# One block of channels in four takes its input product on VectorE instead of through TensorE

## What is computed

```python
dbc = u @ W_x
delta = softplus(dbc[..., :dtr] @ W_dt + b_dt)           # (b, l, 256)
Bm, Cm = dbc[..., dtr:dtr + n], dbc[..., dtr + n:]        # (b, l, 16) each
deltaA = exp(einsum('bld,dn->lbdn', delta, A))
deltaBu = einsum('bld,bln->lbdn', delta * u, Bm)
h[l] = deltaA[l] * h[l-1] + deltaBu[l]
y[l] = einsum('bdn,bn->bd', h[l], C[l])
```

## Time and profile before

| | |
|---|---|
| median of three runs | 519.88 us (516.26 to 520.61) |
| profiled execution, its own time | 519.67 us |
| span of the core in it | 517.9 us, granted TensorE clock 0.938 |
| busy: TensorE, ScalarE, VectorE, GpSimd | 426.4, 334.5, 299.1, 253.7 us |
| first scan starts, last scan ends | 62.9 us, 369.6 us |

### The profile page before, as it was taken

The page is one execution under the profiler, slowest core; times in us unless marked ns, Lnnn a source line. Parts: engine busy times, 40 slices in busy tenths (PEclk is TensorE's granted clock), DMA queues, the critical chain, the costliest instruction groups (busy, mean ns, idle before and its releaser), DMA issues.

```text
span 517.9 us, 6511 instructions
## 1 busy us (share of the span) xinstructions
PE 426.4 (82%) x2021; PEld 255.3 (49%) x2021; DVE 299.1 (58%) x600; ACT 334.5 (65%) x736; POOL 253.7 (49%) x230
## 2 busy tenths in 40 slices
PE   5988888878979869888958688877796888999992
PEld 3432443343445334544524454533384576887881
DVE  0301554558564549855655986789668257553365
ACT  4235689795769795577797386996186298543242
POOL 2001074469555659557667757695654144332012
PEclk9998999989999979899997697989998799999997
DMA  8001700104100102301000412662120000000003
GB/s 249 13 0 46 197 25 22 41 1 120 45 22 20 41 2 51 96 28 34 20 21 2 124 41 103 209 234 107 50 113 1 2 0 1 1 2 1 1 33 130
DMA packets 18710, 29.11 MB, mean 56 GB/s; under 512 B 2698, under 2 KB 10676, under 8 KB 18420
## 3 DMA queue, kind: packets, MB, share of 16 engines
q1 hardware_dynamic: 18676, 28.70, 17.8%
HBM read 22.27 MB, written 2.23 MB: 47 GB/s over the span
## 4 chain that ended last, share of the span: by engine, by line
PE 36%; ACT 15%; issue 9%; DVE 8%; POOL 7%; POOLq 0%; DVEq 0%; ACTq 0%
PE bank L522 6%; ACT loop_buf L1009 6%; PE bank L657 5%; POOL state L1545 4%; PE bank L538 4%; ACT front_a L1019 3%; PE bank L833 3%; DVE state L1171 3%; PE bank L809 3%; PE bank L603 2%; ACT state L1043 2%; ACT state L1044 1%; PE bank L841 1%; PE bank L800 1%; PE bank L612 1%
## 5 line engine op out<-in xcount | busy, mean ns | idle before, releaser
L1171 DVE TENSOR_TENSOR_SCAN state<-front_a,bank 128x512 f32<-128x512 f32 x128 | 151.2, 1209 | 102.2 <-PE bank L522 62.3
L522 PE MATMUL bank<-ident,loop_buf 128*128 128x128 f32 x512 | 90.9, 299 | 40.1 <-ACT loop_buf L1009 33.3
L522 PEld LDWEIGHTS bank<-ident,loop_buf 128*128 128x128 f32 x512 | 63.0, 149 | 109.5 <-issue 37.3
L1009 ACT ACTIVATE loop_buf<-copy,b_rows 128x256 f32<-128x256 f32 x252 | 105.3, 496 | 0.1
L1545 POOL TENSOR_TENSOR state<-state,c_own 128x1024 f32<-128x1024 f32 x32 | 75.2, 2359 | 50.3 <-DVE state L1171 50.3
L1545 POOL TENSOR_TENSOR state<-state,front_a 128x1024 f32<-128x1024 f32 x32 | 79.9, 2510 | 37.9 <-DVE state L1171 37.9
L1019 ACT ACTIVATE front_a<-loop_buf,a_neg 128x512 f32<-128x512 f32 x128 | 84.4, 712 | 10.9 <-DVE state L1171 9.9
L657 PE MATMUL bank<-state,fold 128*64 128x512 f32 x256 | 75.5, 671 | 10.2 <-POOL state L1545 6.1
L538 PE MATMUL bank<-front_c,conv_raw 128*128 128x512 f32 x128 | 60.4, 603 | 2.9 <-ACT front_b L884 1.2
L538 PEld LDWEIGHTS bank<-front_c,conv_raw 128*128 128x128 f32 x128 | 22.9, 195 | 23.7 <-issue 20.4
L1562 POOL TENSOR_TENSOR loop_buf<-state 128x256 f32<-128x256 f32 x24 | 17.8, 742 | 30.3 <-DVE state L1316 30.3
(11 more groups left out here) (197 smaller groups left out, 681.6 us busy)
## 6 DMA issues: line engine op xcount, KB each, us to landing
front_a<-c_stage SPq DMA_DIRECT2D x32, 128.0 KB, 2.9
c_own<-c_stage SPq DMA_DIRECT2D x32, 128.0 KB, 2.9
loop_buf<-front_b SPq DMA_DIRECT2D x32, 128.0 KB, 2.4
copy<-in_L_attn_x SPq DMA_DIRECT2D x4, 512.0 KB, 4.9
front_b<-in_L_ffn_wo SPq DMA_DIRECT2D x1, 2048.0 KB, 9.0
copy<-in_L_ffn_wq SPq DMA_DIRECT2D x1, 2048.0 KB, 9.6
out<-loop_buf SPq DMA_DIRECT2D x3, 512.0 KB, 2.9
conv_raw<-in_L_attn_conv_w SPq DMA_DIRECT2D x2, 512.0 KB, 3.7
```

The source lines that it names most:

```text
L522: return pe.transpose(dst, src, ident[:])
L1009: act.activation(zed[:, g % NZ, c, :, i, :], du_rows[b % 2][:, c, :].rearrange("p (k d) -> p k d", k=2 * KD), ACT.Copy, scale=b_rows[:, b ...
L1171: dve.tensor_tensor_scan(state[:, t % NH, j, :], decay[:, u % NDA, :], bank[BU_BANK[u % NBU]][:], 0.0, ALU.mult, ALU.add).then_inc(scanned, 1)
```

## The change

The fourth block of channels (k = 3, channels 192 to 255) no longer goes through Z and a bank:

- Z has three blocks: each Z activation has 192 elements instead of 256, and TensorE skips `turn_bu` for k = 3. Each of the three banks now belongs to one k, so that `turn_bu(u)` waits for `scan(u - 4)` instead of `scan(u - 3)`.
- VectorE makes the product itself (`make_bu`, L1213 of the new kernel): one 128x512 `tensor_tensor` of `b_wide` and `du_wide`, both in SBUF, in place, once a pair, after the first scan of the pair. The fourth scan reads both of its operands from SBUF.
- `b_wide` holds B broadcast over the partitions: two more transfers of 128 KB for each pair, behind the two for C (`widen_bc`). `du_wide` holds delta*u of the last 64 channels twice: two transfers for each batch (`widen_du`), behind the eight of `widen_delta`.
- To make room `duT` and `x_rows` have one copy instead of two, so that loading x for a batch waits for the transposes of the x before.

```diff
-        silu_r, uT, resT, du_rows, duT, x_rows = ([copies[i][1][j] for i in range(2)] for j in range(6))
+        silu_r, uT, resT, du_rows = ([copies[i][1][j] for i in range(2)] for j in range(4))
+        duT, x_rows = copies[0][1][4:]
...
+        b_wide = copies[1][0][:, 4 * KD * L:].rearrange("p (s l) -> p s l", s=NCW)
...
                 if b >= 1:
                     wait_filled(sp, ("xT1", b - 1))
...
+            def widen_du(b):
+
+                if b >= 2:
+                    sp.wait_ge(bu_made, NPAIR * (b - 1))
+                sp.wait_ge(du_ready, KD * (b + 1))
+                for i in range(2):
+                    sp.dma_start(du_wide[i * P // 2:(i + 1) * P // 2, b % 2, :],
+                                 duT[P // 2:, KD - 1, :]).then_inc(in_du[b % 2], 16)
...
+                if g >= NCW:
+                    sp.wait_ge(scanned, 4 * (g - NCW + 1))
+                for i in range(2):
+                    sp.dma_start(b_wide[i * P // 2:(i + 1) * P // 2, g % NCW, :],
+                                 bc_stage[b, 2 * m + i:2 * m + i + 1, :].partition_broadcast(P // 2)).then_inc(in_b[g % NCW], 16)
...
             def turn_bu(u):
                 g, k = u // 4, u % 4
-                if u >= NBU:
-                    pe.wait_ge(scanned, u - NBU + 1)
+                if k == KZ:
+                    return
+                if g >= 1:
+                    pe.wait_ge(scanned, u - 4 + 1)
...
+            def make_bu(g):
+
+                b = g // NPAIR
+                dve.wait_ge(in_b[g % NCW], 32 * (g // NCW + 1))
+                dve.wait_ge(in_du[b % 2], 32 * (b // 2 + 1))
+                dve.tensor_tensor(b_wide[:, g % NCW, :], b_wide[:, g % NCW, :], du_wide[:, b % 2, :], ALU.mult)\
+                   .then_inc(bu_made, 1)
...
             for t in range(B * NST):
                 scan(2 * t)
+                if t % 2 == 0:
+                    make_bu(t // 2)
                 scan(2 * t + 1)
```

80 lines of the change are left out of this document (50 added, 30 removed).

## The result

| | before | after |
|---|---|---|
| median of four runs each, side by side | 518.14 us (516.26 to 520.61) | 532.50 us (527.46 to 537.47) |
| profiled execution, its own time | 519.67 us | 530.28 us |
| span, granted TensorE clock | 517.9 us, 0.938 | 528.5 us, 0.905 |
| up to the first scan; the loop; behind it | 62.9; 306.6; 148.4 us | 60.65; 318.8; 149.1 us |

The changed kernel is slower: ratio 1.0244, 95% interval 1.0184 to 1.0305 (that it is slower by more than 2% is not shown by this). Ratios here are taken over undisturbed executions only, so one can differ a little from the quotient of two medians. The profiled executions differ by 10.6 us: 2.3 less ahead of the loop, 12.2 more in it, 0.7 more behind it.

What follows compares the result with a forecast made beforehand. No engine was full in the loop: VectorE set ten dense pairs, while in the 22 others scans waited for TensorE and ScalarE. Sum: 519.7 + 2.2 + 16 + 0 - 11 = 526.9, so 527 us; range 510 to 545.

Steps and rivals of the forecast that it cites:

- An added wait for GpSimd: VectorE's product and SBUF scan in the loop wait for a running GpSimd operation; 31.5 us of waits in all.
- Rival (2): In the loop, a scan from SBUF doesn't wait for GpSimd, giving 519.5 us; chance 0.17.
- The product's waits: Behind each pair's first scan, the product waits for GpSimd: 8.4 us over 32 places, product mean 0.95 us.
- The ten dense pairs: Ten loop pairs with VectorE busy 76.2 of 79.5 us; product and waits add 16 us there, between 11.2 and 27.4.
- the end read at the places: Low end for the ten pairs VectorE fills: 14.5 us of product and waits less 3.3 idle, 11.2 us.
- The 22 other pairs: Remaining loop pairs, with 97.7 us of VectorE idle time against 39 us of new work: 0 us added.
- The far end of 13: A third of the 39 us in the 22 pairs is passed on if later scans hold up other engines: 13 us.
- SyncE, 2.2: Ahead of the loop, B's transfers stand before those that widen delta, making the first scan 2.2 us later.
- Removed: Loop work taken from TensorE (22.7 us of transposes) and ScalarE (13.4 us of Z); 11 us gained, between 5 and 25.
- (1): VectorE's idle time in the loop swallows the new work, so the kernel gets faster, 510 us; chance 0.16.
- (3): VectorE and GpSimd become the bound in every loop pair, 7.75 us before front or tail work; 551 us, chance 0.15.
- (4): The product waits for its transfers at three batch starts, 3 us or so each; 536 us, chance 0.07.

Runs made afterwards that it cites:

- full_path: Changed kernel with nothing removed: Z has four blocks, all transposes are made, product and SBUF scan stay, B has two slots; ratio to before 1.0442.
- product_only: Same as `full_path`, but the fourth scan reads its bank again, so the product is made and not used; ratio to before 1.0133.
- after_again: The changed kernel itself, unaltered, timed once more beside `to_bank`; 535.48 us, ratio to before 1.0309.
- to_bank: Changed kernel with the product written into the PSUM bank the pair's first scan has just read, and the fourth scan reading it there; 520.37 us, ratio 0.9989.
- slot: Changed kernel with the last two scans of a pair exchanged, so the SBUF scan is third; ratio to before 1.0218.
- x_late: Kernel before, with only the load of x of batch 1 moved behind the router weights and the first transpose of x; 520.45 us.
- b_behind: Changed kernel with B's first transfers, for four pairs, issued behind those that widen delta; ratio to before 1.0226.
- to_bank_late: As `to_bank`, with the product one place later, directly behind the second scan; 519.83 us, ratio to before 1.0051.

## Why the prediction was right, and where its sum was not

The direction, the range and the mechanism were right: 527 forecast, 510 to 545, slower at 0.54; 530.28 in the profiled execution and 532.5 by the median. That the number came so near is in part luck. The loop was to grow by 16 + 0 - 11 = 5 us and grew by 12.2; the first scan was to come 2.2 us later and came 2.3 earlier, by a clock that was not forecast; behind the loop 0.7 came in. 7.2 - 4.5 + 0.7 is the 3.4 us between 526.9 and 530.3. By its steps:

**"An added wait for GpSimd"** is shown, and for the scan too. Forecast were means of 1.9 us for SBUF scans and 1.21 for the others, measured 1.925 and 1.209. `full_path` against `product_only` and `after_again` against `to_bank` put the scan's wait at 16 and 15 us, the largest single part of the change. Rival (2), that a scan from SBUF doesn't wait, is refuted. The rule weighed there, from "SBUF — State Buffer" of the Trainium skill, section "Who interferes with whom", holds here for a scan with 2.55 us beside a `weigh` of 2.36 and 1.20 without one. The runs add that of two instructions which one release sets free together VectorE's can come first, as at 132.33 in `slot`.

**The product's waits** were read as 8.4 us at fixed places and are 38.6 - 32 x 0.668 = 17.2. The scans' came out at 61.6 - 32 x 1.20 = 23.2 against 23.1. The places moved: in a stretched pair a `weigh` begins with each first scan, and the product finds half of it left, as in the pair at 137.80. The mean was to be 0.95 and is 1.21.

**The ten dense pairs, 16**: the term is for the added work alone, and so `full_path`, which removes nothing, measures it: 13.0 (6.0 for the product, 6.9 for the SBUF scan). The changed kernel's 10.8 has 2.2 of the removal in it. So the end read at the places, 11.2, was too low and 16 too high; of the 4.8 added for growth 1.8 was needed. The settled form of 7.7 us was nearly reached by short pairs with little front or tail work, while the pairs of 14.3 us, full of such work, grew by only 0.2.

**The 22 other pairs, "I take 0"**, is the term that failed. It said that the idle time there covers the new work. With it and the removal the changed kernel's came out at +1.4. The removal itself is worth 7 to 10 us (11 forecast), 7.7 of them in these pairs by the table. So the new work costs some 9 us there (`full_path`, +9.2), of which 1.3 are the product's and 7.9 the SBUF scan's. The 9 is an upper figure: pair 5 alone has 3.2 of it, and grew by 2.3 in `x_late`, without any new work. The far end of 13 stood in the text, with its mechanism: engines that are held up in turn by later scans. An idle time of 4.4 us a pair, on the average, hid much of the new work, but a scan that ends 1.3 us late frees its decay slot, its bank and its `weigh` 1.3 us late wherever the idle time lies. The waits for VectorE and `weigh` grow along with it (us, from the groups of each page):

| | before | product_only | full_path | after |
|---|---|---|---|---|
| decays for scans | 9.9 | 12.4 | 16.7 | 23.2 |
| transposes for scans | 6.6 | 12.2 | 14.4 | 15.3 |
| `add_states` for `weigh` | 6.1 | 5.2 | 9.2 | 11.8 |
| `add_states` for `gT` | 4.1 | 5.0 | 8.5 | 11.1 |

That these waits carry the 9 us, and in what shares, is argued from their growth, not isolated. One of the prediction's own signs of being wrong, that the long pairs grow too, came true in part: of the eleven pairs among the 22 that were over 10 us long, six grew, by 0.5 to 3.2, and five became 0.1 to 0.5 shorter.

**SyncE, 2.2**: the widening of delta did start late, 52.91 where delta was ready at 50.55, and the order of the start is as forecast:

```profile
52.91 5.08 SPq L468 DMA_DIRECT2D loop_buf<-front_b  x8
...
58.03 1.24 SPq L477 DMA_DIRECT2D loop_buf<-copy  x2
...
59.83 1.33 ACT L1048 ACTIVATE front_a<-loop_buf,a_neg 128x512 f32<-128x512 f32 x2 [3.52 <-DMA loop_buf<-front_b]
...
60.65 1.22 DVE L1205 TENSOR_TENSOR_SCAN state<-front_a,bank 128x512 f32<-128x512 f32 x1 [4.45 <-ACT front_a L1048]
```

The first decay waits for that transfer. `b_behind` gives 1.7 back. But the first scan came at 60.65, not 65.1, in an execution whose prologue had the higher clock earlier and longer. A start 4.5 us earlier in `x_late` left the whole where it was, so I don't book this as a gain of the change; that an early start is always given back is argued from that one kernel. `du_wide` was at no cost: no product waited for it in the changed kernel.

**Removed**: TensorE's transposes lost 15.6 us (90.9 to 75.3), not 22.7, since each takes 314 ns instead of 299; `add_states` went from 671 to 724 ns and the convolution from 603 to 630, against these rows of before:

```profile
L657 PE MATMUL bank<-state,fold 128*64 128x512 f32 x256 | 75.5, 671 | 10.2 <-POOL state L1545 6.1
L538 PE MATMUL bank<-front_c,conv_raw 128*128 128x512 f32 x128 | 60.4, 603 | 2.9 <-ACT front_b L884 1.2
```

This goes with the granted clock, 0.93 to 0.88 in the loop, of which the prediction warned without a price; what it costs by itself wasn't isolated. ScalarE's Z lost exactly the 54 ns of each (496 to 442). In the loop TensorE's busy time fell by 2.9 us where 20 were named, ScalarE's by 12.0 where 13 were, and VectorE's rose by 58 where 50 were.

**The other rivals.** (1) fell: the idle time didn't swallow it. (3) came true for the form of a settled pair, 7.71 us, but not for the whole: 328.8 us of loop in `full_path` are 22 above before, where it has 27.4 + 13. (4) fell: the product's group has 0.0 us of idle time before it.

The sum with the measured terms, in the loop, dense pairs first: +6.0 + 1.3 for the product, +6.9 + 7.9 for the SBUF scan, -9.9 for the removal = +12.2. The terms are differences of the same four loops, so that they add up proves nothing; `to_bank` is the independent check of the SBUF scan's.

## What to carry to other kernels

Work moved to an engine that idles a third of the time is not free if its results release others: here up to 9 of the 22 us that VectorE's new work cost came from pairs with idle time, so price the wait of whoever is released, not only the busy pairs. Before moving an operand of a VectorE instruction from PSUM to SBUF, look at what GpSimd does at that moment: the bank was worth 15 us for 32 scans. Putting the SBUF scan elsewhere (`slot`) made it shorter and the kernel no faster, because GpSimd's consumer then waited; giving the scan a PSUM operand ended its wait.

## What the hardware showed unasked

A `tensor_tensor_scan` of 128x512 in float32 takes 1.18 to 1.22 us whether its second operand lies in SBUF or in PSUM, and longer beside GpSimd only in the first case: up to 2.77 us in the changed kernel and 3.44 in `slot`, never over 1.22 from a bank. A product of the same size takes 0.67 us alone, into SBUF or into a bank (`to_bank_late`), and 0.70 in `to_bank`, where it waits for the scan just ahead of it. And the same 16 matmuls in the prologue took 10.10 us before and 7.11 in the changed kernel, the first seven at half speed in the one and none in the other, and the first scan came 4.5 us earlier in `x_late` with nothing to show for it at the end.
